# Wg0's high and low part as one 256-column moving operand, in a two-stage graph network on one core

## The reference, cut to what matters

```
def _L1_gnn_ref(x, adj, Wg0, bg0, Wg1, bg1, Wih, Whh, bih, bhh):
    h = relu(einsum('ts,bsh->bth', adj, x @ Wg0 + bg0))
    h = relu(einsum('ts,bsh->bth', adj, h @ Wg1 + bg1))
    for p in range(1, 5):                       # windows of p nodes
        nw = T // p
        wins = h[:, :nw * p].reshape(B * nw, p, H)
        last = lstm_last(Wih[p-1], Whh[p-1], bih[p-1], bhh[p-1], wins)
        h = h.at[:, arange(nw) * p + (p - 1)].set(last)
    return h
x = layernorm(x + L0(x, adj * adj, W1, W2, W3))
x = layernorm(x + L1(x, adj, ...))
```

## Time and profile before

| | |
|---|---|
| median of 3 runs | 983.25 us |
| profiled execution | 983.22 us, span 981.5 us |
| PE, DVE, ACT, POOL busy | 98%, 66%, 44%, 4% of the span |
| granted clock of PE, mean | 0.996 |
| Wg0 products (L1265) | 192, 22.8 us |
| chain that ended last | PE 95% |

### The profile page before, as it was taken

How to read it: one execution, slowest core, us unless ns; L and a number is a source line. 1 busy time by engine, 2 the same in 40 slices (tenths; PEclk the granted TensorE clock), 3 DMA queues, 4 the chain that set the end, 5 groups by cost and what they waited for, 6 DMA issues and landing times.

```text
span 981.5 us, 14408 instructions
## 1 busy us (share of the span) xinstructions
PE 966.2 (98%) x5279; PEld 846.3 (86%) x5279; DVE 650.9 (66%) x1442; ACT 429.9 (44%) x788; POOL 35.2 (4%) x34
## 2 busy tenths in 40 slices
PE   9999999999999999999999999999999999999994
PEld 7888998889888898888988898898988889898894
DVE  7765557454575545754766656877776786877987
ACT  6353403433044331352434445455454555455765
POOL 0000200002000020000000001001010000100000
PEclk9999999999999999999999999999999999999998
DMA  8000000101011010104600000000000000000001
GB/s 306 1 1 1 13 32 18 69 1 44 0 43 43 0 43 1 61 26 143 232 2 0 1 1 1 0 2 22 1 1 22 0 22 0 22 1 22 1 1 65
DMA packets 11287, 31.01 MB, mean 32 GB/s; under 512 B 1120, under 2 KB 2400, under 8 KB 11232
## 3 DMA queue, kind: packets, MB, share of 16 engines
q1 hardware_dynamic: 11232, 30.30, 8.4%
HBM read 22.95 MB, written 7.34 MB: 31 GB/s over the span
## 4 chain that ended last, share of the span: by engine, by line
PE 95%; DVE 3%; ACT 1%; issue 1%; DVEq 0%; ACTq 0%
PE ps L1192 24%; PE ps L848 19%; PE ps L824 11%; PE ps L826 11%; PE ps L825 11%; PE ps L1030 9%; PE ps L1245 3%; PE ps L1265 2%; PE ps L866 2%; PE ps L1113 1%; PE ps L1022 1%; PE ps L1307 1%; DVE stats L1689 1%; PE ps L1339 1%; PE ps L1308 0%
## 5 line engine op out<-in xcount | busy, mean ns | idle before, releaser
L848 PE MATMUL ps<-adj,t 128*128 128x512 f32 x480 | 112.9, 390 | 0.0
L848 PEld LDWEIGHTS ps<-adj,t 128*128 128x128 f32 x480 | 89.3, 188 | 18.0
L1030 PE MATMUL ps<-s,adj 128*128 128x256 f32 x768 | 94.1, 284 | 0.0
L1030 PEld LDWEIGHTS ps<-s,adj 128*128 128x128 f32 x768 | 92.6, 192 | 0.0
L824 PE MATMUL ps<-adj,node 128*128 128x512 f32 x216 | 84.5, 391 | 0.1
L826 PE MATMUL ps<-adj,node 128*128 128x512 f32 x216 | 84.3, 390 | 0.0
L825 PE MATMUL ps<-adj,node 128*128 128x512 f32 x216 | 84.3, 390 | 0.0
L1610 ACT ACTIVATE gates_x<-ps,lb 128x258 f32<-128x258 f32 (+1 forms) x156 | 66.5, 508 | 40.3 <-PE ps L1192 40.2
L1610 ACT ACTIVATE gates<-ps,lb 128x512 f32<-128x512 f32 (+2 forms) x117 | 66.7, 647 | 37.9 <-PE ps L1192 28.7
L848 PE MATMUL ps<-sx,t 128*128 128x512 f32 x360 | 83.2, 389 | 0.0
L848 PEld LDWEIGHTS ps<-sx,t 128*128 128x128 f32 x360 | 67.6, 188 | 14.0
(11 more groups left out here) (250 smaller groups left out, 1819.2 us busy)
## 6 DMA issues: line engine op xcount, KB each, us to landing
xb<-in_x SPq DMA_DIRECT2D x7, 1024.0 KB, 4.9
sx_raw<-in_adj_t SPq DMA_DIRECT2D x8, 512.0 KB, 8.6
adj_raw<-in_adj_t SPq DMA_DIRECT2D x8, 512.0 KB, 7.8
out<-xb SPq DMA_DIRECT2D x7, 512.0 KB, 2.6
xn<-xb SPq DMA_DIRECT2D x3, 1024.0 KB, 4.0
xb<-xn SPq DMA_DIRECT2D x6, 512.0 KB, 6.9
xb<-in_x SPq DMA_DIRECT2D x2, 512.0 KB, 5.4
lw_raw<-in_wih_t SPq DMA_DIRECT2D x1, 1024.0 KB, 11.3
```

The source lines that it names most:

```text
L848: last = pe.matmul(dst, t7[:, B_BLOCK[v], a, tile], A_BLOCK[v](b, t), start=start and t == 0 and (a, b) == (HI, HI), stop=t == QUARTER - 1 ...
L1030: last = pe.matmul(dst, adj[:, a, m, nt:nt + P], s3[:, b, m, :, :].rearrange("p j c -> p (j c)"), start=(m == 0 and t == 0 and (a, b) == ( ...
```

## The change

From the third element on (slot 2), z's high part multiplies both parts of Wg0 at once: a moving operand of 256 columns, high and low part side by side, with the results side by side in PSUM. z's low part multiplies Wg0's high part as before, into the columns of the high part. A half then fills two banks, 6 and 7, whichever half it is. DVE adds the two: columns of the low part plus the bias into `node_raw` (SBUF), then the columns of the high part to that; ACT's relu and DVE's relu-subtract read `node_raw`. banks_of makes bank_free respect both banks. In the lists, `wg0 0` and `wg0 1` no longer stand together: X 3,2 comes between them, and `step(Y, 1, 0, BANK)` comes ahead of `adj_h 0`. In DRAIN the last tile of `adj_x 1` comes ahead of `wg0 0`.

```diff
+        def side_by_side(slot):
+            return slot >= 2
+        def banks_of(slot, name, half):
+            return {GB, GB + 1} if name == "wg0" and side_by_side(slot) else {bank_of(slot, name, half)}
...
-                ("adj_x", 1, 0, 8), step(X, 3, 1), ("wg0", 0), ("wg0", 1), ("ahead",), step(X, 3, 2),
-                ("adj_h", 0, 0, 4), ("adj_h", 0, 4, 8), ("ahead",), step(X, 4, 0), ("ahead",),
-                step(Y, 1, 0, BANK), ("ahead",), step(X, 4, 1), ("ahead",), ("adj_h", 1, 0, 6),
+                ("adj_x", 1, 0, 8), step(X, 3, 1), ("wg0", 0), ("ahead",), step(X, 3, 2), ("wg0", 1), ("ahead",),
+                step(Y, 1, 0, BANK), ("adj_h", 0, 0, 4), ("ahead",), step(X, 4, 0), ("adj_h", 0, 4, 8),
+                ("ahead",), step(X, 4, 1), ("ahead",), ("adj_h", 1, 0, 6),
...
-                    held = [u for u in mine[:unit_at(slot, name, i)] if bank_of(slot, *u) == bank_of(slot, name, i)]
+                    held = [u for u in mine[:unit_at(slot, name, i)] if banks_of(slot, *u) & banks_of(slot, name, i)]
...
+                            for i in (HI, LO):
+                                if i == HI:
+                                    hi_reached(b_lo_of(slot, "adj_x", v))
+                                else:
+                                    lo_reached(b_lo_of(slot, "adj_x", v))
+                                for t in range(4):
+                                    nt = (4 * v + t) * P
+                                    dst = ps[:, GB + t // 2, t % 2 * 2 * F:t % 2 * 2 * F + (2 * F if i == HI else F)]
+                                    last = pe.matmul(dst, z[:, i, nt:nt + P],
+                                                     wgs[:, :, 0, :] if i == HI else wgs[:, HI, 0, :],
+                                                     start=(t % 2 == 0 and i == HI), stop=(i == LO),
+                                                     skip_group_check=True)
...
+                        src = node_raw[:, cols] if wide else ps[:, bank_of(slot, *item[:2]), :]
+                        nc.scalar.activation(node[:, HI, cols], src, ACT.Relu).then_inc(b_hi, 1)
...
+                            nc.vector.tensor_tensor(raw, part_of_w(LO), bias, ALU.add).then_inc(bias_add, 1)
+                            dve.wait_ge(bias_add, ahead("bias", slot, turn, 2 * item[1] + 1))
+                            nc.vector.tensor_tensor(raw, part_of_w(HI), raw, ALU.add).then_inc(bias_add, 1)
+                            hi_ready(b_lo_of(slot, "wg0", item[1]))
+                            lo_relu(node[:, LO, cols], node_raw[:, cols], node[:, HI, cols], b_lo)
```

More of the change, by code:

```diff
@@ L466, in build @@
         DRAIN = [("ahead",), ("stats", 0, 8, 3), ("adj_x", 0, 0, 8), step(Y, 1, 0), ("adj_x", 1, 0, 7),
-                step(X, 3, 0), ("wg0", 0), ("adj_x", 1, 7, 8), step(X, 3, 1), step(Y, 1, 0, BANK, held=True),
+                step(X, 3, 0), ("adj_x", 1, 7, 8), ("wg0", 0), step(X, 3, 1), step(Y, 1, 0, BANK, held=True),
                 ("wg0", 1), ("root", 0, 8, 3), step(X, 3, 2), ("scale", 0, 8, 3), ("adj_h", 0, 0, 7),
@@ L565, in build @@
             "lo": lambda n: (B_MM + splits(n)) * (n < B),
-            "bias": lambda n: 2 * (n < B),
+            "bias": lambda n: (4 if side_by_side(n) else 2) * (n < B),
             "gate": lambda n: sum(len(gates_of(u.s)) for u in steps_of(n)),
@@ L1256, in pe_slot @@
                         bank_free("wg0", v)
+                        if side_by_side(slot):
+                            for i in (HI, LO):
[10 more added lines that the diff above has]
+                                                     skip_group_check=True)
+                            last.then_inc(b_mm, 1)
+                            continue
                         for i, j in ((HI, HI), (HI, LO), (LO, HI)):
@@ L1640, in act_slot @@
                     elif item[0] == "wg0":
-                        act.wait_ge(bias_add, ahead("bias", slot, turn, item[1] + 1))
-                        nc.scalar.activation(node[:, HI, cols], ps[:, bank_of(slot, *item[:2]), :], ACT.Relu).then_inc(b_hi, 1)
+                        wide = side_by_side(slot)
+                        act.wait_ge(bias_add, ahead("bias", slot, turn, (2 if wide else 1) * (item[1] + 1)))
+                        src = node_raw[:, cols] if wide else ps[:, bank_of(slot, *item[:2]), :]
+                        nc.scalar.activation(node[:, HI, cols], src, ACT.Relu).then_inc(b_hi, 1)
                     elif item[0] == "adj_h" and item[3] == MT:
@@ L2255, in dve_slot, with part_of_w @@
                         dve.wait_ge(b_mm, ahead("mm", slot, turn, unit_at(slot, "wg0", item[1]) + 1))
+                        if side_by_side(slot):
+                            def part_of_w(j):
+                                return ps[:, GB:GB + 2, :].rearrange("p b (t j c) -> p b t j c", t=2, j=2)[
+                                    :, :, :, j, :].rearrange("p b t c -> p (b t) c")
+                            raw = node_raw[:, cols].rearrange("p (t c) -> p t c", c=F)
+                            bias = bias0[item[1]][:].rearrange("p (t c) -> p t c", c=F)
+                            nc.vector.tensor_tensor(raw, part_of_w(LO), bias, ALU.add).then_inc(bias_add, 1)
[3 more added lines that the diff above has]
+                            lo_relu(node[:, LO, cols], node_raw[:, cols], node[:, HI, cols], b_lo)
+                            continue
                         unit = ps[:, bank_of(slot, *item[:2]), :]
```

## The result

The changed kernel takes 1023.24 us (median of 4 runs, 1022.08 to 1024.63) against 983.26 (4 runs, 983.07 to 983.37): a ratio of 1.0407, 95% interval 1.0389 to 1.0425. That is 40 us slower, where 36 were forecast (1018.9, range 1010 to 1029).

A forecast was written before the change was run, and what follows sets the result against it. PE was taken as the bound, busy 98% of the span. Six slots' savings and added waits, slots 2 to 6 27.7 us and DRAIN 2.5, make 30.2 (1013.4); with 5.5 for the clock 1018.9 us, range 1010 to 1029.

The forecast's parts named there:

- products, both halves: Wg0 on PE: both halves' products take 1.86 us instead of 2.62, 0.76 us less per slot.
- first wait, X 3,2: PE in X 3,2, before its state products, waits 0.18 us for the high part of the step before from DVE.
- second wait, Wg0's second half: PE waits 1.37 us until the first half's low part is written, since the second half writes both banks.
- third wait, adj_h 0: PE waits 4.74 us for bank 6, until the second half's low part leaves DVE, behind X 3,2's cell.
- clock, per slot: PE's clock falls to half in two of five long stalls, 2.7 us each: 5.5 us in all.
- nothing is given back later in the slot: PE's work queued behind adj_h 0's wait was waiting for nobody, so slots 2 to 6 lose 5.53 us each.
- The strided adds: DVE's two adds per half, reading columns 128 apart from two banks: 0.69 us taken, bounds 0.60 and 0.79.
- DRAIN's first wait: Slot 7: Wg0's first half, behind adj_x 1's last tile, waits some 3 us for that result's low part.
- the walk: The prediction's step-by-step passage through slot 3 and DRAIN, keeping the durations of the trace before the change.
- DRAIN's sum: Slot 7: 2.69 us later at the first half, 0.38 gained, 0.17 at adj_h 0; together 2.5 us.
- my second rival: The clock falls at each long stall: 983.2 + 30.2 + 13.6 = 1027 us; chance 0.12.
- My first: Rival: the stalls come and the clock stays, 1013.4 us; chance 0.32.

The follow-up runs named there:

- e3: The changed kernel, but Wg0's banks count as free once DVE's second add has read them, not when the low part is written: 1018.12 us.
- e4: The changed kernel with slot 7 as before the change (separate products, a bank per half, old DRAIN list): 1019.24 us.
- e5: The changed kernel plus 18 unread products of 512 columns ahead of adj_h 0 in slots 2 to 6, keeping PE at work: 1014.67 us.
- e2: The changed kernel with the lists of before the change for slots 2 to 6, DRAIN as changed: 1021.07 us.
- e6: The changed kernel, but on DVE and ACT Wg0's second half stands ahead of X 3,2's cell and gates in slots 2 to 6: 1005.34 us.

## Why the prediction was right, and where it was off

Slot 3 from the start of Wg0 to X 4,0, start to start, after against before:

| step of the prediction | forecast | measured |
|---|---|---|
| products, both halves | -0.76 | 0.87 + 0.97 - 2.62 = -0.78 |
| first wait, X 3,2 | 0.18 | 650.10 - 647.84 - 2.01 = 0.25 |
| second wait, Wg0's second half | 1.37 | 653.37 - 650.10 - 1.89 = 1.38 |
| third wait, adj_h 0 | 4.74 | 660.96 - 654.34 - 2.06 = 4.56 |
| clock, per slot | 1.1 (5.5 over five) | 665.14 - 660.96 - 12 x 0.229 = 1.43 |
| sum | 6.6 | 6.84 |

The products and the three waits held within 0.2 us each, and the order, places and releasers of the waits held too. The second and the third are, by e3, one delay of adj_h in two parts: both hang on DVE's list, and without the second the third would be longer by as much. That nothing is given back later in the slot held too: five slots of 6.84 are 34.2 of the 38.7 us by which the span grew, and DRAIN has most of the rest, by e4 about 4.0.

The strided adds, for which no row existed, took 0.67 to 0.69 us, the value taken; ACT's relu from SBUF 0.63.

DRAIN's first wait came out at 905.47 - 902.13 - 0.23 = 3.11 us, by the walk 3.12. DRAIN's sum was 2.5, and e4 measured 4.0: the step that failed there is that I gave it no fall of the clock, while X 3,1's twelve input products took 3.27 us instead of 2.01:

```profile
905.47 1.42 PE L1273 MATMUL ps<-wgs,z 128*128 128x256 f32 x8 [2.96 <-DVE z L1696]
906.69 3.43 PE L1199 MATMUL ps<-hw,lw 128*128 128x344 f32 x12
909.96 2.05 PE L1199 MATMUL ps<-hstep_x,lw 128*128 128x344 f32 x12
```

This fall does not always come. In e3's profile PE stands the same 2.96 us at the same place, and the clock stays at 1.00:

```profile
903.35 1.13 PE L1275 MATMUL ps<-wgs,z 128*128 128x256 f32 x8 [2.96 <-DVE z L1698]
```

```profile
901.00:909.00 8.00, 5.65 (x36) 5.52 (x37) 4.65 (x9) 2.95 (x7) 0.00 (x0) 1.00 0.00 0
```

The mis-sized term is the clock's. I took two falls of 2.7 us. The profiled execution has six, one at each long wait, and each costs about 1.4 us: in the five slots the low stretch begins within the wait, and under 3 us of it meet products. 5.5 forecast, 5 x 1.43 + about 1.5 = 8.7 measured. Of the number and the price of the falls one was too low and the other too high, and the two errors partly cancel; that part of the total is luck. What came is, in kind, my second rival, a fall at every long stall, to which I gave 0.12: it had the five falls of the slots right and their price too high. My first, that the clock stays, is refuted by the six rows at 0.72 and by e5.

The profiled execution is the fastest of the four, 1.2 us below the median. The runs now spread over 2.5 us, where those of before spread over 0.3. Low stretches of two lengths would give such a spread, and e4's profile has both, in slots whose lists are those of the change: 6.8 us at the lower level in slots 2 and 3, 3.4 in the other three. Its slots 3 and 4:

```profile
659.00:669.00 10.00, 6.42 (x23) 5.32 (x24) 5.30 (x8) 3.62 (x7) 0.00 (x0) 0.66 0.00 0
726.00:736.00 10.00, 7.86 (x32) 6.52 (x33) 5.07 (x10) 4.63 (x9) 0.00 (x0) 0.83 0.00 0
```

The mean granted clock of the change's runs fits: 0.986 in the two near 1022 us, 0.984 and 0.983 in the two above 1024. That these two had the longer stretches at the same waits is not shown, since only one run was profiled; nor does a run show what decides between the two lengths.

## What to carry to other kernels

Where one engine is busy without a gap, a saving on it is worth its size and so is every wait added to it; before widening an operand, count the banks its result holds, and for how long. Walk the list of the engine that frees them: here 0.8 us of products a slot were bought with 6.2 us of waits, because a sum of 2.8 us was queued behind a cell of 5.7. Where several waits of one engine hang on the same list, the last one decides: taking an earlier one away only lengthens it (e3). And the stalls here cost more than their length, because the products behind them ran at the lower clock.

## What the runs showed that was not expected

Four products of 256 and four of 128 columns stand 0.109 us apart on average (0.87 us for eight), as 24 of 128 columns did: in this place the wider ones cost no more, though the 768 of the earlier trace rows are busy for 0.1225 each.

In DRAIN the clock fell after PE was back at work: PE is idle until 905.47, the granted clock is 1.00 up to 906 and 0.58 from there to 907. Slow products can thus follow a wait of 3 us although the first of them still ran at 2.4 GHz. It was so in e4's slots 4 to 6 too: in slot 4 PE is back at 728.14, and the clock falls between 728.5 and 728.75. For DRAIN:

```profile
905.00:906.00 1.00, 0.53 (x4) 0.53 (x5) 0.42 (x1) 0.00 (x0) 0.00 (x0) 1.00 0.00 0
906.00:907.00 1.00, 1.00 (x7) 1.00 (x7) 0.07 (x1) 0.00 (x0) 0.00 (x0) 0.58 0.00 0
```

Over the profiles of the change, e2, e3 and e4 the clock fell in or just behind each of the 20 stalls of 4.3 us and more, five in each. Of the five stalls of about 3.0 us in DRAIN (the change, e2, e3, e5, e6) all but e3's had a fall, and none of the waits of 0.8 to 1.2 us in e6's slots had one.

Adding 90 products that nobody reads made the kernel 8.6 us faster (e5 against the change): adj_h starts no earlier, and the clock no longer falls in slots 2 to 6.
